# The four batches of a convolution-attention hybrid written out instead of looped over

## The reference

```python
x = x + conv_attention(group_norm(x))            # 4 heads of 32; softmax over 4096 keys
t = x as tokens
t = t + linear_attention(layer_norm(t))          # softmax over d for q, over tokens for k; 128x128 context
t = t + expert_mixture(layer_norm(t))            # 8 experts, top 2, weights renormalised
```

## Time and profile before

| | |
|---|---|
| median of 3 runs | 3085.73 us (3085.62 to 3086.46) |
| the profiled execution: its time / its span | 3086.66 us / 3084.8 us |
| mean granted TensorE clock | 0.967 of full speed |
| busy: PE / DVE / ACT / POOL | 2896.0 / 2571.0 / 2407.3 / 706.3 us |
| instruction queues (fetch): packets, MB | 182, 2.98 and 174, 1.43 |

### The profile page before, as it was taken

How to read it: one execution, slowest core, us unless ns; L and a number is a source line. 1 busy time by engine, 2 the same in 40 slices (tenths; PEclk the granted TensorE clock), 3 DMA queues, 4 the chain that set the end, 5 groups by cost and what they waited for, 6 DMA issues and landing times.

```text
span 3084.8 us, 62037 instructions
## 1 busy us (share of the span) xinstructions
PE 2896.0 (94%) x20374; PEld 1031.1 (33%) x20374; DVE 2571.0 (83%) x3579; ACT 2407.3 (78%) x3132; POOL 706.3 (23%) x726
## 2 busy tenths in 40 slices
PE   6999999988899999998989999999898999999988
PEld 3222222275422222237532222223743222222474
DVE  5888888878788888887878888888787888888877
ACT  4999999744699999974479999996447999999634
POOL 1122221114322221111422222121152222122115
PEclk9999999998999999999999999999899999999989
DMA  2655555500165556550025565554002555555300
GB/s 81 121 110 110 110 111 110 97 1 15 57 120 109 112 110 114 97 97 1 21 63 111 112 114 108 107 110 83 1 21 50 110 110 111 109 106 113 71 1 28
DMA packets 72164, 257.83 MB, mean 84 GB/s; under 512 B 8160, under 2 KB 10240, under 8 KB 71808
## 3 DMA queue, kind: packets, MB, share of 16 engines
q0 software_dynamic: 64512, 234.91, 40.3%
q1 hardware_dynamic: 7296, 18.51, 1.6%
HBM read 10.12 MB, written 8.39 MB: 6 GB/s over the span
## 4 chain that ended last, share of the span: by engine, by line
PE 71%; issue 11%; DMA 7%; DVE 5%; ACT 2%; POOL 1%; POOLq 0%; SPq 0%; ACTq 0%; DVEq 0%
PE BK L1071 70%; DMA RM<-EA 7%; DVE X L1042 2%; ACT KE L536 1%; PE BK L1076 1%; POOL KE L459 1%; ACT PVC L515 0%; DVE X L1034 0%; ACT XT L545 0%; DVE ST L703 0%; ACT EA L536 0%; DMA WEXP<-in_L_ffn_expert_w 0%; PE BK L1344 0%; SPq L342 0%; DVE XT L782 0%
## 5 line engine op out<-in xcount | busy, mean ns | idle before, releaser
L835 DVE TENSOR_TENSOR XT<-XT,KE 128x512 f32<-128x512 f32 x1344 | 1567.5, 1227 | 167.9 <-ACT KE L536 167.1
L536 ACT ACTIVATE KE<-BK 128x512 f32<-128x512 f32 (+1 forms) x1536 | 1488.1, 1022 | 126.0 <-PE BK L1071 38.9
L1071 PE MATMUL BK<-Q,K 32*128 32x512 f32 x8192 | 1169.1, 640 | 15.5 <-ACT KE L536 10.0
L1071 PE MATMUL BK<-KE,V 128*32 128x512 f32 x6144 | 815.0, 604 | 0.0
L418 POOL DMA_DIRECT2D RM<-EA x448 | 392.3, 934 | 1510.1 <-ACT KE L536 637.1
L1071 PEld LDWEIGHTS BK<-Q,K 32*128 32x128 f32 x8192 | 321.2, 182 | 871.3 <-ACT KE L536 627.0
L536 ACT ACTIVATE EA<-BK 128x512 f32<-128x512 f32 (+1 forms) x512 | 497.1, 1025 | 28.2
L1071 PEld LDWEIGHTS BK<-KE,V 128*32 128x32 f32 x6144 | 125.3, 108 | 577.4 <-ACT KE L536 503.6
L1071 PE MATMUL BK<-EA,V 128*32 128x512 f32 x2048 | 272.6, 604 | 0.0
L1071 PE MATMUL BK<-WEXP,XT 128*128 128x512 f32 x512 | 237.8, 611 | 16.5 <-DVE X L1042 16.5
L615 ACT ACTIVATE RM<-BK,GT 128x128 f32<-128x128 f32 x512 | 145.9, 368 | 132.8 <-PE BK L1071 132.8
(11 more groups left out here) (168 smaller groups left out, 1866.8 us busy)
## 6 DMA issues: line engine op xcount, KB each, us to landing
RM<-EA POOLq DMA_DIRECT2D x224, 768.0 KB, 6.6
RM<-EA POOLq DMA_DIRECT2D x224, 256.0 KB, 3.3
XN<-in_x SPq DMA_DIRECT2D x16, 512.0 KB, 6.5
out<-X SPq DMA_DIRECT2D x16, 512.0 KB, 2.6
WEXP<-in_L_ffn_expert_w SPq DMA_DIRECT2D x1, 512.0 KB, 6.6
CONST<-in_consts SPq DMA_DIRECT2D x1, 384.0 KB, 5.6
WQKV<-in_L_conv_w_qkv SPq DMA_DIRECT2D x1, 192.0 KB, 2.1
WQKV<-in_L_attn_W_qkv SPq DMA_DIRECT2D x1, 192.0 KB, 5.8
```

Source lines behind the costliest of these rows:

```text
L536: nc.scalar.activation(exps(jt, p), scored(c * T + jt, p).rearrange("p a n -> p (a n)"), ACT.Exp, scale=SCALE0).then_inc(s_exp, 1)
L835: v.tensor_tensor(acc, acc, exps(jt, p), ALU.add).then_inc(s_adds, 1)
L1071: return nc.tensor.matmul(o, lhsT, rhs, start=start, stop=stop, skip_group_check=shared)
```

## The change

Every `Fori` over the batches becomes a Python loop, so the body stands four times in each engine's program and b is a constant in each. The tests on b at 382 and 1090 become Python tests and leave nothing in the program. The tests of the flag stay, four times per engine, with the same path first as before.

```diff
-            with sp.Fori(0, batches - 1) as b:
+            for b in range(batches - 1):
...
-            with pool.Fori(0, batches) as b:
+            for b in range(batches):
...
-                with pool.If(b):
+                if b:
...
-            with act.Fori(0, batches) as b:
+            for b in range(batches):
...
-            with dve.Fori(0, batches) as b:
+            for b in range(batches):
...
-            with pe.Fori(0, batches) as b:
-
-                with pe.If(b):
+            for b in range(batches):
+
+                if b:
```

## The result

The changed kernel takes 3076.58 us (median of 8 runs, 3075.11 to 3078.65), the kernel before 3086.10 (8 runs, 3085.17 to 3090.42). The ratio is 0.9963, with a 95% interval of 0.9954 to 0.9973: it is faster by 0.37% by this ratio; the two medians are 9.5 us apart, which is 0.31%. The forecast was 3084.3, within 3079.5 to 3090.0, and "no change" with a chance of 0.82. It was wrong.

A forecast was written before the change was run, and what follows sets the result against it. TensorE was taken to bound the steady tile (71% of the chain's span), with 0.26 us of slack to ScalarE. Gains of 5.4 less losses of 4.0 made 1.4 us faster than 3085.73: 3084.3, range 3079.5 to 3090.

The forecast's parts named there:

- The late wait: ScalarE's head-0 exponentials: the wait for scores becomes a separate instruction, 0.07 us later each, 48 places, 3.4 us lost.
- The rival that it eats the slack: Steady attention tiles: a separate wait beyond 0.26 us of slack slows some 900 tiles; 3131 at 0.30 us; chance 0.06.
- The step on TensorE: First scores after V and first group-mean matmul of each batch: last wait moved ahead, 8 x 0.08, 0.6 us lost.
- Register steps on TensorE, VectorE and ScalarE cost nothing: Register instructions computing wait values run hidden on these three engines, so removing them gains zero.
- the rival of 65 us: TensorE's 2032 register steps of 32 ns come off whole, giving 3021, or half, giving 3053; chance 0.09.
- The meetings: Three places where batches meet: without VectorE's jump and the steps before the transposes, 2.0 us gained.
- Without the jump I expect 1.64 everywhere: At each meeting, the aggregate starts 1.64 us after the last transpose, as in batch 0; 0.31, 0.57 and about 0.55 gained.
- The steps ahead of the transposes: At each meeting, a register step and the loop head's bases go before the transposes, 0.2 us gained each.
- The start: Kernel start, before the first transposes: loop entry and the test of b go, 0.6 us gained.
- GpSimd's transfers: Accumulating transfers in each batch's last chunk: register steps go from the links and a wait turns, 2.4 us gained.
- The 0.4 us: Last add of the kernel, 0.1 for its turned wait, and batch 0's first-chunk transfers, 0.3: 0.4 us gained.
- the register rival: Register steps were on the path, so removing them makes the kernel faster, to 3021 or 3053; chance 0.09.

The follow-up runs named there:

- VectorE alone: Only VectorE's four batches written out in the kernel before, the other engines keeping their loops: 3084.14 us, ratio 0.9983.
- ScalarE alone: Only ScalarE's four batches written out in the kernel before, the other engines keeping their loops: 3088.72 us, ratio 0.9997.

## Why the prediction was wrong, point by point

- **The late wait**: right. 0.07 us were taken, 0.08 measured, and it disappears in the steady tile (2.07 us, exponentials 1.24 us behind the scores) and counts at the first five tiles (1.89 us) and at each later chunk. 3.4 us were predicted; turning the wait back gave 4.1 between the medians and 3.7 in the traces. The rival that it eats the slack was priced off 0.30 us and is out. The step on TensorE was real as well (0.09 at the first scores).
- **Register steps on TensorE, VectorE and ScalarE cost nothing**: not contradicted. The steady tile is 2.07 us in every kernel, and the rival of 65 us is out.
- **The meetings**: the jump was right, its size was not. 2.0 us were predicted and 4.75 came. The step that failed is "Without the jump I expect 1.64 everywhere": in the change the aggregate starts 2.44 us after the last transpose, and the transposes end 1.7 us sooner. I took the 1.64 us from last transpose to aggregate from batch 0, where the transposes themselves ran at 213 ns each, the pace of the low clock, and carried it to meetings that had the low clock too. Where the low clock stayed and only the jump went, in the last meeting of the kernel with VectorE alone, it is indeed 1.64 us. At full clock the transposes end earlier, VectorE is then bound by its own 5.03 us of statistics, and the earlier start counts in full: the statistics start 1.1 us after the transposes and not 2.3 to 2.6, and VectorE's idle time before them is 1.25 us, where 1.7 was forecast. In the kernel before, the low clock in the transposes cost nothing, since the jump was the later of the two. That the clock was at full in all meetings of the change had no part in the forecast, and some 0.9 us or more of each meeting hang on it. The steps ahead of the transposes gave 0.25 us each, against 0.2 taken.
- **The start**: 0.2 to 0.6 us from the traces of these two kernels, against 0.6; the first transposes were forecast near 19.1 and stand at 19.2 and 19.5. Over the traces without added instructions they start at 19.2 to 19.5 with TensorE written out (six) and at 19.7 to 20.1 with its loop (five), 0.6 us apart on average. The 2.0 us in batch 0's transposes are the clock's, and no part of the program was needed for them.
- **GpSimd's transfers**: the term that broke the range. 2.4 us were predicted, 6.2 to 8.5 came, and the step that failed is the reading of the chain as register steps plus a transfer of fixed length. The steps are there (1.48 us a link before and 1.34 after, where 1.59 and 1.43 were read and forecast), but they are not what the merge waited for: with all of them kept and the fetches moved, the merges took 23.8 us. Without this term's excess of 3.8 to 6.1 us the time would have been at 3080.4 to 3082.7, an estimate from the traces, and inside the range. The trace of before had the varying part in it, landings of 6.6 us in the median and 8.2 at the fourth for transfers of one size, and I did not ask what made the slow ones slow. Had the packets been laid beside TensorE's fetches, the exposure would have been visible: an edit that shifts TensorE's instructions can move it. Over all 14 traces the four merges take 23.5 to 31.9 us together.
- **The 0.4 us** for the last add and for batch 0's first chunk: no run isolates them.
- **The net**: 5.4 gained and 4.0 lost were predicted. The traces have 11.1 to 13.8 gained at these places (start 0.2 to 0.6, meetings 4.8, merges 6.2 to 8.5) and 2.8 to 4.6 lost, and 2.0 more by the clock in batch 0.
- **The rivals**: none of them held this case. The chance of 0.11 for faster went to the register rival, which is false; the faster result came from a mechanism that had no place in the list.

Not settled: why the change's mean clock is higher (0.972 on average against 0.969), and how much time that is worth beyond the places named. Why ScalarE alone moves TensorE's fetches by 3 to 5 us stays open; a request that meets an engine already busy with the transfer would be held behind it, so that a small shift could flip the order. The many fetches that start in the last 0.15 us of a transfer fit this, but it is only argued.

## What to carry to other kernels

Unrolling changes more than jumps: look at which wait stays on the operation (with constants, here, the first one called), and call the one that ends last first; this alone was worth about 4 us of 3077. Where a chain of dependent transfers sets the end of a stage, lay the instruction fetches beside it before pricing anything else, and take a duration at a meeting only from an occurrence with the same granted clock. A forecast that rests on one trace should take in what two traces of the same kernel differ by, here 3.7 us.

## What the runs showed of the hardware that I had not expected

- A fetch of 16 KB of instructions by TensorE lengthens an accumulating transfer of 768 KB: from first to last packet it takes 4.02 us in the median without a fetch, 5.20 with one at its head and 4.44 with one at its end. The fetch is a single packet of 1.06 us on average. That it does so by holding one of the 16 engines while the transfer ends with its last packet fits these numbers, but the traces do not name the engine of a packet. 64 semaphore instructions at the start of a program (they moved the fetches by some 3 to 4 us, where two are some 15.6 us apart, so about a quarter of a packet) took away 6 to 8 us at the merges in the traces, while the median time fell by 0.9 us, which is not clear of noise.
- A taken jump was expensive wherever the traces have one on VectorE or GpSimd: 2.5 to 3.1 us from the branch to the next instruction, back to a loop's head and over the general path alike. The change keeps the second kind.
- The written-out program fetched fewer packets than the looped one (168 and 104, against 182 and 174). It executes fewer instructions (52362 against 62037), and loops presumably fetch their bodies anew in every batch; the latter was not tested.
- A semaphore instruction with nothing to wait for took TensorE 0.15 us from start to start: 64 of them ran from 1.0 to 10.6 us, 128 from 1.0 to 20.4 and 182 from 1.0 to 28.7. The first matmul stood at 13.6 us in the kernel before, so the 64 were covered and most of the rest was not.
